# The router's dot products move from VectorE to TensorE, the output products are made in place, and two of thirteen input products leave GpSimd

## The reference, cut to what matters

```python
xh = layernorm(x)                                   # [16, 1024, 512]
xp = xh @ x_proj_w.T                                # 64 ranks, 16 B, 16 C
delta = softplus(xp[..., :64] @ dt_proj_w.T + dt_b)
h = exp(delta * A) * h_before + delta * B * xh      # for each channel and state, along the tokens
x1 = x + sum_n(h * C) + xh * D                      # y is the sum over states, with the skip term
weights = layernorm(x1) @ router_w + router_b       # one number a token; the top 255 of 2048 go on
```

## Time and profile before

| | us |
|---|---|
| median of three runs | 4458.69 (4455.69 to 4460.14) |
| the profiled execution | 4463.26 |
| its span, first to last instruction | 4461.5 |
| scanning part, to the last router weight | about 3465 |
| DVE, POOL, ACT, PE busy in the span | 3768.9, 3363.5, 2861.0, 3066.8 |

### The profile page before, as it was taken

How to read it: one execution, slowest core, us unless ns; L and a number is a source line. 1 busy time by engine, 2 the same in 40 slices (tenths; PEclk the granted TensorE clock), 3 DMA queues, 4 the chain that set the end, 5 groups by cost and what they waited for, 6 DMA issues and landing times. The chain is left out here.

```text
span 4461.5 us, 61468 instructions
## 1 busy us (share of the span) xinstructions
PE 3066.8 (69%) x17574; PEld 1408.3 (32%) x17574; DVE 3768.9 (84%) x3027; ACT 2861.0 (64%) x4425; POOL 3363.5 (75%) x1716
## 2 busy tenths in 40 slices
PE   4667665766676666665665756666664289999997
PEld 1222232322232222222232323222222145555553
DVE  2999999999999999999999999999998754555552
ACT  5777777777778687868777777777774223332221
POOL 3999999999999999999999999999998100000010
PEclk7767676767766676667676767676775589999998
DMA  4454546463646455554545464636453300000000
GB/s 102 104 136 121 148 114 158 96 170 87 171 101 156 114 144 130 127 136 122 134 123 135 124 152 105 164 84 180 92 146 76 144 22 20 19 19 19 19 19 8
DMA packets 198219, 472.94 MB, mean 106 GB/s; under 512 B 60688, under 2 KB 61200, under 8 KB 197088
## 3 DMA queue, kind: packets, MB, share of 16 engines
q1 hardware_dynamic: 177136, 452.11, 40.3%
q0 software_dynamic: 20736, 16.88, 1.4%
HBM read 126.83 MB, written 73.43 MB: 45 GB/s over the span
## 5 line engine op out<-in xcount | busy, mean ns | idle before, releaser
L955 POOL TENSOR_TENSOR ch<-hid,cmat 128x1024 f32<-128x1024 f32 x1024 | 2385.4, 2358 | 92.7 <-DVE hid L821 76.4
L821 DVE TENSOR_TENSOR_SCAN hid<-place,inp 128x1024 f32<-128x1024 f32 x1024 | 2266.1, 2270 | 105.4 <-ACT place L671 87.3
L671 ACT ACTIVATE place<-delr,a_neg 128x1024 f32<-128x1024 f32 x1024 | 1126.8, 1111 | 293.6 <-DVE hid L821 190.2
L444 PE MATMUL ps_y<-ch,nsum 128*32 128x256 f32 x8192 | 856.5, 517 | 424.3 <-POOL ch L955 423.4
L810 DVE TENSOR_TENSOR inp<-place,bmat 128x1024 f32<-128x1024 f32 x816 | 941.6, 1211 | 64.2 <-ACT place L677 63.4
L455 PE MATMUL ps_y<-ident,ysb 128*128 128x128 f32 x1024 | 319.2, 408 | 599.0 <-ACT ysb L684 580.0
L444 PEld LDWEIGHTS ps_y<-ch,nsum 128*32 128x32 f32 x8192 | 254.6, 137 | 1025.6 <-POOL ch L955 753.2
L917 POOL TENSOR_TENSOR inp<-dxr,bmat 128x1024 f32<-128x1024 f32 x208 | 490.2, 2357 | 0.0
L455 PEld LDWEIGHTS ps_y<-ident,ysb 128*128 128x128 f32 x1024 | 230.5, 278 | 807.9 <-ACT ysb L684 759.1
L1216 POOL DMA_INDIRECT out_rows<-row,idx_out x16 | 41.1, 2571 | 532.3 <-issue 298.4
L439 PE MATMUL ps_y<-xhT,dskip 128*32 128x256 f32 x2048 | 260.8, 600 | 134.2 <-ACT xr L691 134.2
(11 more groups left out here) (176 smaller groups left out, 4202.8 us busy)
## 6 DMA issues: line engine op xcount, KB each, us to landing
dxr<-dxT SPq DMA_DIRECT2D x1024, 128.0 KB, 2.4
delr<-delT SPq DMA_DIRECT2D x1024, 128.0 KB, 2.4
xr<-in_x SPq DMA_DIRECT2D x32, 1024.0 KB, 6.6
bmat<-b_and_c SPq DMA_DIRECT2D x256, 128.0 KB, 3.4
cmat<-b_and_c SPq DMA_DIRECT2D x256, 128.0 KB, 3.1
x_rows<-xr SPq DMA_DIRECT2D x16, 2048.0 KB, 7.7
out_rows<-xr SPq DMA_DIRECT2D x32, 1024.0 KB, 5.1
w<-in_w SPq DMA_DIRECT2D x2, 4096.0 KB, 24.4
```

The source lines that it names most:

```text
L444: last = pe.matmul(ps_y[q * CH:(q + 1) * CH, 0:2 * P], nsum[:], ch[:, g, q * 2 * P:(q + 1) * 2 * P], start=False, stop=(g == GROUPS - 1))
L671: nc.scalar.activation(place[:, PLACE[par, c, g], :], delr[:, c % 2, :], ACT.Exp, scale=a_neg[:, i:i + 1])\
L821: nc.vector.tensor_tensor_scan(hid[:, g, :], place[:, PLACE[par, c, g], :], inp[:, g, :], 0.0, ALU.mult, ALU.add).then_inc(hid_ready, 1)
L955: nc.gpsimd.tensor_tensor(ch[:, g, :], hid[:, g, :], cmat[:, g, :], ALU.mult).then_inc(ch_ready, 1)
```

## The change

1. Router, x part. The projection's weights get 32 more columns, all of them the router's row, so that 32 rows of the projected state hold the router's product with the normalised x. PE brings row 96 of it to token rows by eight matmuls of one column (`router_x`, chunk 14), ACT copies them, POOL undoes the norm's scale (`scale_route_x`, after (15, 1)).
2. Router, y part. `ysb` keeps all 16 chunks' sums; 16 matmuls for each of two token halves, with four columns, take their product with the router's row (`router_y`, after the sums of (0, 0) and (0, 1) of the next batch). ACT copies them (`copy_router_y`, chunk 0, place 3), and `route` puts the parts together with five operations. DVE's router goes, and so do the waits for it.
3. The output product is written over the states in `hid`; `ch` goes. The scan waits for PE's sum instead of POOL's product; POOL's wait for the sum goes.
4. `OWN_AT` ends at chunk 11: DVE makes group 3's input for chunks 12 and 13.
5. Three things move: the step-size sums by PE, one POOL product from (2, 3) to (3, 1), and the small constants.

```diff
-         (2, 3): (0, 2, 3), (7, 3): (0, 3, 3)}
-ADD_TERMS = {(2, 0): ((0, 2), (0, 3), (1, 1)), (2, 1): ((1, 1), (1, 2), (2, 1)),
+         (3, 1): (0, 2, 3), (7, 3): (0, 3, 3)}
+ADD_TERMS = {(2, 0): ((0, 3), (1, 0), (1, 3)), (2, 1): ((1, 3), (2, 0), (2, 3)),
-RW_COPY = (2, 1)
-ROUTER = (2, 3)
+ROUTE_Y = ((0, 0), (0, 1))
+COPY_ROUTE_Y = (0, 3)
+ROUTE_X = (14, 0)
+COPY_ROUTE_X = (14, 3)
+SCALE_ROUTE_X = (15, 1)
-OWN_AT = tuple(range(1, 14))
+OWN_AT = tuple(range(1, 12))
...
+            def router_x(b):
+                aux_free(b, ("route_x",))
+                for t in range(TC):
+                    last = pe.matmul(aux[:, t:t + 1], xpT[R + 2 * N:P, t * P:(t + 1) * P],
+                                     ident[R + 2 * N:P, R + 2 * N:R + 2 * N + 1], start=True, stop=True)
+                last.then_inc(aux_full, 1)
+            def router_y(b, t, emptied):
+                if t == 0:
+                    pe.wait_ge(aux_emptied, emptied)
+                for c in range(CHUNKS):
+                    last = pe.matmul(aux[:, 4 * t:4 * t + 4], ysb[:, c, t * P:(t + 1) * P], rw_chunk[:, c, :],
+                                     start=(c == 0), stop=(c == CHUNKS - 1))
+                if t == 1:
+                    last.then_inc(route_y_full, 1)
...
                 pe.wait_ge(ch_ready, tile(b, c, g) + 1)
-                                     ch[:, g, q * 2 * P:(q + 1) * 2 * P],
+                                     hid[:, g, q * 2 * P:(q + 1) * 2 * P],
...
+                        if (c, g) in ROUTE_Y and has(b, 1):
+                            router_y(b - 1, ROUTE_Y.index((c, g)), b * NUSE + USE["z", 2, 1] + 1)
+                        if (c, g) == ROUTE_X and not final:
+                            router_x(b + 1)
...
+            def copy_router_y(b):
+                if has(b, 1):
+                    act.wait_ge(wcol_ready, b)
+                act.wait_ge(route_y_full, b + 1)
+                nc.scalar.activation(route_y[:].rearrange("p (q t) -> p t q", t=2),
+                                     aux[:, 0:TC].rearrange("p (t q) -> p t q", t=2), ACT.Copy)\
+                    .then_inc(route_y_copied, 1)
...
-                nc.scalar.activation(ysb[:], ps_y[:, 0:2 * P], ACT.Copy).then_inc(ysb_ready, 1)
+                if c == 0 and has(b, 1):
+                    act.wait_ge(route_y_full, b)
+                nc.scalar.activation(ysb[:, c, :], ps_y[:, 0:2 * P], ACT.Copy).then_inc(ysb_ready, 1)
...
             copy_x1(last, 1, CHUNKS - 1)
-            copy_rw(last, nb_run * NUSE)
+            copy_router_y(last)
             ln2_sums(last, 1, range(17))
...
                 if has(b, 1) or c > 0:
-                    dve.wait_ge(ch_ready, tile(b, c, g) - GROUPS + 1)
+                    dve.wait_ge(ch_summed, tile(b, c, g) - GROUPS + 1)
...
-                    if has(b, 1) and c in ROUTER:
-                        router(b - 1, other, ROUTER.index(c))
...
+            def scale_route_x(b, par):
+                ...
+                nc.gpsimd.tensor_tensor(route_in[:, par, 1, :], m1[:, 1, :], rw_sum[:].to_broadcast([P, TC]), ALU.mult)\
+                    .then_inc(route_in_step, 1)
+                nc.gpsimd.tensor_tensor(route_in[:, par, 0, :], route_x[:], r1[:, 7, :], ALU.mult)\
+                    .then_inc(route_in_step, 1)
+                pool.wait_ge(route_in_step, n + 2)
+                nc.gpsimd.tensor_tensor(route_in[:, par, 0, :], route_in[:, par, 0, :], route_in[:, par, 1, :],
+                                        ALU.subtract).then_inc(route_in_step, 1)
...
-                        if has(b, 1) or c > 0:
-                            pool.wait_ge(ch_summed, tile(b, c, g) - GROUPS + 1)
-                        nc.gpsimd.tensor_tensor(ch[:, g, :], hid[:, g, :], cmat[:, g, :],
+                        nc.gpsimd.tensor_tensor(hid[:, g, :], hid[:, g, :], cmat[:, g, :],
                                                 ALU.mult).then_inc(ch_ready, 1)
```

More of the change, by code:

```diff
@@ L67 @@
 OWN = GROUPS - 1
-OWN_AT = tuple(range(1, 14))
+OWN_AT = tuple(range(1, 12))
 ROUTED = (4, 2)
 STORE_LOAD = (3, 4)
-USES = [("xhat", t) for t in range(TC)] + [("proj", 0), ("proj", 1)] + [("z", k, h) for k in range(2) for h in range(2)] \
+USES = [("xhat", t) for t in range(TC)] + [("proj", 0), ("proj", 1)] + [("z", k, h) for k in range(2) for h in range(2)] + [("route_x",)] \
     + [(stage, k, h) for k in (2, 3) for stage in "zs" for h in range(2)]
@@ L77 @@
 NUSE = len(USES)
-LN1 = 5
-LN2 = 7
+LN1 = 6
+LN2 = 6
+ROUTE_STEPS = 4
 LN_ACT = 20
@@ L146, in scan_phase @@
         rb = sb("rb", [P, 1])
+        rw_chunk = sb("rw_chunk", [P, CHUNKS, 4])
+        rw_sum = sb("rw_sum", [P, 1])
+        route_x = sb("route_x", [P, TC])
+        route_in = sb("route_in", [P, 2, 2, TC])
+        route_y = sb("route_y", [P, TC])
+        route_t = sb("route_t", [P, 3, TC])
         xr = sb("xr", [P, 2, TC, D])
@@ L403, in project @@
                 for k in ks:
-                    last = pe.matmul(aux[0:R + 2 * N, :], xproj[:, k, :],
+                    last = pe.matmul(aux[:], xproj[:, k, :],
                                      xhT[:, xhat_slot(k, par)[0], xhat_slot(k, par)[1], h * HALF:(h + 1) * HALF],
@@ L423, in add_terms @@
                     aux_free(b, ("s", k, h))
+                    if (k, h) == (2, 0) and has(b, 1):
+                        pe.wait_ge(route_y_copied, b)
                     pe.wait_ge(z_act, b * KD * ZACT + k * ZACT + ZACT)
@@ L454, in turn_y @@
                     x_t = xr[:, par, :, c * CH:(c + 1) * CH].rearrange("p (q t) d -> p t q d", t=2)[:, t]
-                    pe.matmul(out_t, ysb[:, t * P:(t + 1) * P], ident[:], start=True, stop=False)
+                    pe.matmul(out_t, ysb[:, c, t * P:(t + 1) * P], ident[:], start=True, stop=False)
                     last = pe.matmul(out_t.rearrange("p (q d) -> p q d", q=4), ident[:], x_t, start=False, stop=True)
@@ L501, in _ @@
             turn_y(nb_run - 1, 1, CHUNKS - 1)
+            for t in range(2):
+                router_y(nb_run - 1, t, nb_run * NUSE)
             pe.wait_ge(wcol_ready, nb_run)
-            pe.wait_ge(aux_emptied, nb_run * NUSE)
+            pe.wait_ge(route_y_copied, nb_run)
             pe.transpose(aux[0:nb_run * TC, 0:P], wcol[:, 0:nb_run * TC], ident[:]).then_inc(wt_ready, 1)
@@ L703, in _ @@
             act.wait_ge(eps_ready, 1)
+            nc.scalar.activation(squares[:, 1, 1], rw[:], ACT.Identity, accum_out=rw_sum[:]).then_inc(rw_summed, 1)
+            act.wait_ge(rw_summed, 1)
             ln1_sums(0, 0, range(17))
@@ L864, in _ @@
             batches(dve, body)
-            last = nb_run - 1
-            for h in range(2):
-                router(last, 1, h)
             dve.wait_ge(wt_ready, 1)
@@ new lines, in route @@
+            def route(b, par):
+                n = b * ROUTE_STEPS
+                pool.wait_ge(ln2, b * LN2 + LN2)
+                pool.wait_ge(route_y_copied, b + 1)
+                pool.wait_ge(route_in_step, b * 3 + 3)
+                if has(b, 1):
+                    pool.wait_ge(wcol_ready, b)
+                nc.gpsimd.tensor_tensor(route_t[:, 0, :], m2[:, 1, :], rw_sum[:].to_broadcast([P, TC]), ALU.mult)\
+                    .then_inc(route_step, 1)
+                nc.gpsimd.tensor_tensor(route_t[:, 1, :], route_y[:], route_in[:, par, 0, :], ALU.add)\
+                    .then_inc(route_step, 1)
+                pool.wait_ge(route_step, n + 2)
+                nc.gpsimd.tensor_tensor(route_t[:, 2, :], route_t[:, 1, :], route_t[:, 0, :], ALU.add)\
+                    .then_inc(route_step, 1)
+                pool.wait_ge(route_step, n + 3)
+                nc.gpsimd.tensor_tensor(route_t[:, 1, :], route_t[:, 2, :], r2[:, 4, :], ALU.mult)\
+                    .then_inc(route_step, 1)
+                pool.wait_ge(route_step, n + 4)
@@ L967, in body @@
                         if (c, g) == ROUTED and has(b, 1):
-                            route(b - 1)
+                            route(b - 1, 1 - par)
+                        if (c, g) == SCALE_ROUTE_X and not final:
+                            scale_route_x(b + 1, 1 - par)
                     if c + 1 in OWN_AT:
@@ L975, in _ @@
                     delta(0, 0, k, step)
+            scale_route_x(0, 0)
             batches(pool, body)
             ln2_finish(nb_run - 1)
-            route(nb_run - 1)
+            route(nb_run - 1, 1)
     return out_done
@@ L1823 @@
         "router_w": np.broadcast_to(i["L0_ffn_router_w"].reshape(1, D), (P, D)),
+        "router_chunk": np.stack([np.concatenate([i["L0_ffn_router_w"].reshape(CHUNKS, CH).T if q == j
+                                                  else np.zeros((CH, CHUNKS), np.float32) for q in range(4)])
+                                  for j in range(4)], axis=2),
         "router_b": np.broadcast_to(i["L0_ffn_router_b"].reshape(1, 1), (P, 1)),
```

77 lines of the change are left out of this document (39 added, 38 removed).

## The result

The changed kernel takes 4611.68 us (median of 4 runs, 4607.88 to 4612.74) against 4457.62: ratio 1.0344, interval 1.0326 to 1.0362. My forecast was 4520, with a range up to 4595; the time lies above it, next to the rival that I called low clock (4605, chance 0.15).

The account below looks back on a forecast made before the run. DVE (96% busy) and POOL (97%), both nearly full, and the chain between them bound it; +3.2 a batch, 48 us for 15, with 1.4 + 2.3 + 9.3 gave +61: 4524, or 4520 on the median's footing; range 4430 to 4595.

Parts of the forecast that it names:

- low clock: Rival: clock at 0.50 during the y part's loads, 0.213 us a record, +8.5 a batch, 4605 us; chance 0.15.
- the y part: Chunks 0 and 1: ACT's copy waits for 64 new TensorE records at 0.13 us each, +3.7 us a batch.
- 64p - 4.6: ACT's new wait at the end of chunk 0, p being the time per record: 3.7 us at p = 0.13.
- the sum: Per batch -6.1 + 2.3 + 1.2 + 3.7 + 2.1 = +3.2 us, 48 us for 15 batches.
- my term of 8.3: The y part's 64 TensorE records a batch at 0.13 us each, 8.3 us.
- Router off DVE: Chunks 2 and 3: four products of 3.02 us leave DVE after each, -6.1 us a batch.
- Two inputs: Chunks 12 and 13: DVE makes a fourth input, 1.13 us each, +2.3 us a batch.
- In place: End of chunk 15: the scan waits 0.8 us for TensorE's sum, costing nothing by itself.
- x part: End of chunk 15 and the boundary: small POOL operations and ACT's copy delay ACT's sequence, +1.2 us a batch.
- POOL without its pause: Chunks 2 to 4: POOL falls 4.3 us behind, making ACT late before chunks 6 and 7, +2.1 us a batch.
- Ends: Outside the 15 batches: head +1.4, first batch's inputs +2.3, tail +9.3 us (8.0 copy delay, 1.3 longer route).
- the signs that I had named: Trace: ACT idle 2 to 5 us, chunks 0-1 32 to 35, 2-3 12.1 each, POOL trailing 4 to 6, 32 loads 3.5 to 5.

Follow-up runs that it names:

- the third run: The changed kernel with input 3 of chunks 12 and 13 made on GpSimd again: 4560.64 us, ratio 1.0230 to the kernel before.
- the run with two of GpSimd's moves: The changed kernel with the router's last steps moved from (4,2) to (9,2) and a delta from (3,1) to (5,1): 4582.70 us, ratio 1.0268.
- the run with short products: The kernel before with VectorE's eight dot products a batch cut to 8 of 512 columns each: 4407.98 us, ratio 0.9879.

## Why the prediction was wrong

*The step that failed* is in the y part: "In this batch the clock was at 2.4 GHz from 1775.3 to 1785.5, after a dense stretch that stays ...: I take 0.13 a record". The mechanism, ACT's copy waiting for the records, was right, and the size was not: the records take 0.216 in all 15 boundaries. With that, my own 64p - 4.6 gives 9.2 us for ACT's wait where the sum had 3.7 (measured 9.6), and the sum is -6.1 + 2.3 + 1.2 + 9.2 + 2.1 = +8.7 a batch, against 8.74 on average and 9.08 in batches 2 to 14. That it comes so close is in part luck: terms that were off by 0.5 to 0.7 cancel in part. Where the clock did rise, with 128 columns, the wait was the 3.7 of the forecast. I took the rise in the earlier trace rows as belonging to the place. TensorE's timeline of the kernel before has, across that rise, the skip matmuls and two sums of 256 moving columns back to back, and behind it a step with 512:

```profile
1774.14 1.63 PE L444 MATMUL ps_y<-ch,nsum 128*32 128x256 f32 x16
...
1777.16 1.13 PE L426 MATMUL aux<-dxT,ident 128*128 128x512 f32 x2 [0.41 <-ACT tu L581]
```

The change puts its 4-column matmuls behind the first of these sums and ahead of the second. So the dense stretch did not stay, as I wrote it did; the clock was still at 0.50 when the new matmuls began, and with 128 columns in them it rose, with 4 it did not. The pace that I was near to exists, 0.11 a record in first bursts of six boundaries of the third run and two of the run with two of GpSimd's moves, and even there the clock fell back before the burst was done, so that my term of 8.3 would have been 4.0 + 7.0 at best. What it is about the 4 columns that leaves the clock low, no run shows.

By the Trainium skill, TensorE: Matmul & The Clock Gate, section "LDWEIGHTS (loading the stationary operand)", the formula for a load has its columns and no granted clock in it; for 128 columns it gives an estimate of 107 ns. The runs show a record near that at 2.4 GHz (0.11) and twice that at 1.2 GHz (0.216); the measurement decides.

*Router off DVE:* -6.27 for -6.1, and the run with short products shows that such a gain arrives nearly whole when the pause is not all taken. *Two inputs:* +2.26 for +2.3, shown twice by undoing it. *In place:* nothing, as said. *x part:* 1.2 was too much; with the y part cut to one matmul, chunks 0 and 1 are 0.1 longer than before, and chunks 13 to 15 half a microsecond. *POOL without its pause:* the lag at the end of chunk 4 grew from 1.1 to 4.8 us, 3.7 where I had 4.2, and chunks 6 and 7 +2.79 for +2.1; where ScalarE's squares stay in place, the one grows with the other, roughly (table above). *Ends:* head 2.7 for 1.4, batch 0 3.4 for 2.3, tail 12.4 for 9.3, where ACT's copy waits 13.12 for 64 records in 13.77 us, the same slow pace.

I gave the low clock 0.15 and ended the range under its time. Its evidence, 12 us at 0.50 ahead of the place with TensorE busy in half of them, deserved more than the rise that came after the place where the new matmuls begin. Of the signs that I had named, two are in the trace (chunks 2 and 3 at 12.1 each, GpSimd's products of chunk 4 trailing by 4.8); the boundary (38.45 us for 32 to 35), ACT's wait (9.6 for 2 to 5) and the 32 loads (6.9 for 3.5 to 5) are not as I had them.

## What to carry to other kernels

Price a chain of new matmuls of a shape that no row has at both granted clocks, and keep the lower one in the range: the clock that the displaced work had reached did not carry over, and eight of the new bursts that began at 2.4 GHz did not keep it. Where the weights are wide and the moving side narrow, try the operands the other way round (here 14.0 us of TensorE a batch became 3.5, 140 us of the run). Before taking work off the fullest engine, find who caught up during it: here GpSimd ended up 3.6 us later than before, and 2.8 of VectorE's 6.3 us were lost again a few chunks further on. Three moves (squares later, twice, and inputs to VectorE) that helped the chunks they were meant for were paid back, nearly or in full, in others, so judge a move by the batch.

## What had not been expected of the hardware

TensorE was busy without a gap from 1845.4 to 1860.3 in batch 8, with 64 records of 4 moving columns and one sum, and was granted 1.2 GHz throughout; with 128 columns in the same place it went to 2.4 GHz within the first 32 records of the boundary shown. In all eight cases seen, a burst of 4-column matmuls that began at 2.4 GHz (0.11 us a record) fell to 1.2 GHz before its 32 records were done, and the next burst ran at 1.2 GHz throughout (6.99 us); with 128 columns no burst that began at 2.4 GHz fell.
